# Batch 0's own table of window matmuls, constant products in TensorE's pauses, and the first maxima placed from two queues

## The chip, the cores and the metric

The kernel runs on one core of one Trainium2 chip. The metric is the device time of one execution in microseconds (us), as the median of several runs. In profile rows PE is TensorE's matmul side and PEld its weight loads, DVE is VectorE, ACT is ScalarE, POOL is GpSimd, SP is SyncE; SPq and ACTq are the DMA issues of SP's and ACT's instruction queues.

## The reference, cut to what matters

The whole is one gated cross-attention layer and one mixture-of-experts layer over 16 batches. What the change touches lies in the attention:

```python
# x: (16, 256, 128), ctx: (16, 1601, 128), 16 heads of width 8
qh = einsum('bnd,hde->bhne', layernorm(x), Wq)
kh = einsum('bmd,hde->bhme', ctx, Wk)
vh = einsum('bmd,hde->bhme', ctx, Wv)
att = softmax(einsum('bhne,bhme->bhnm', qh, kh) * 0.125)
out_h = einsum('bhnm,bhme->bhne', att, vh)
...
x = x + tanh(g) * (concat(out_h) @ Wo.T)
x = x + tanh(g2) * moe(layernorm(x))      # top 2 of 8 experts
```

## The kernel before

**Two passes over the scores.** The softmax needs the maximum of each query's row of scores over the 1601 context positions. The kernel computes the scores twice. The first pass makes them with queries on the partitions, in windows of 402 positions: `maximum(G, m)` on TensorE is a pair of `window` matmuls (L770), one for each of two row groups, into one of two PSUM buffers `mxp`, and VectorE reduces the pair with one TENSOR_REDUCE (L1501). A group G is four heads of one batch and has NMX = 16 such pairs; there are 64 groups, four in each batch, and so 1024 pairs. After the 16 pairs of a group VectorE makes the negated maxima `nmx` (L1509), GpSimd splits them into three bfloat16 parts (`split_maxima`, L635 to L641), TensorE turns them (`turn_maxima`, L809), ScalarE copies them to `mxT` (`copy_maxima`, L1122), and two DMAs on SP's queue place them as three more rows of `qpack` (`place_maxima`, L437). The second pass makes the scores with context positions on the partitions (`scores`, L748); those three rows subtract the maximum inside the matmul. ScalarE takes the exponential (L1069), and TensorE multiplies by the values (`weighted`, L796, two units later).

**Units.** The second pass goes in units: 13 tiles of the context for each group, 52 units in a batch, 832 in all. Unit u issues its scores, the windows that a hand-written table `WINDOWS_AT` gives it, and the weighted sums of unit u-2. The table has two rows for each unit: the first pair of row 0 is interleaved with the unit's scores, the pairs of row 1 come after the weighted sums. `issued(u, p)` says how many pairs are out before part p of unit u. In batch 0 some 23 pairs are made ahead of unit 0, and the lead over the table grows from 23 to 30 (`LEAD - max(0, SHORT - u // 3)`); in the other batches it is 30. The same table serves all batches. TensorE's instructions run in program order, and the first unit of each group (units 0, 13, 26, 39 of a batch) waits until the maxima of its group are placed.

**The front.** Ahead of unit 0 TensorE makes keys, queries and the values of batch 0 (`keys` L854, `queries` L838, `values` L868), and then pauses until the keys and queries have been packed by DMA (L383, L389). Between the first 23 pairs it makes the queries and the values of batch 1, whose tiles of 128 positions go four to a PSUM bank (`VCH`).

**SP's queue.** SP issues its DMAs in one written-out order. For the front: packing of batch 0's group 0, context of batch 1, packing of group 1 (12 DMAs), two DMAs of ones (L453), packing of group 2 (12), the maxima of group 0 (2), packing of group 3 (12), packing of batch 1's queries (12, L389), four small loads, two DMAs of ones, the rows of batch 2 (L442). Then comes its loop over the units, in which the maxima of group 1 are placed at unit 9, group 2 at unit 23, group 3 at unit 35, and batch 1's keys are packed at units 14, 23 and 35. At unit 7 ScalarE's `first_keys` of batch 1 waits until all four groups of batch 0 are packed.

Of the kernel before, what the change touches and what calls it, by code (L numbers as in the profile page):

```python
# [16 lines left out]
B, N, D = 16, 256, 128  # L17
# [76 lines left out]
X1_AHEAD, Q1_AHEAD, V1_AHEAD = 1, 2, 8  # L94
# [5 lines left out]
LEAD, SHORT = 30, 7  # L100
WINDOWS_AT = ("1011011110111111111111101001101110011111110111100111",
              "1101111020000000000001101211100011100000011000120000")
PER_BATCH = NG * NMX
ISSUED = [sum(int(WINDOWS_AT[q][r]) for r in range(UNITS) for q in range(2) if 2 * r + q < c)
          for c in range(2 * UNITS)]
# [6 lines left out]
def issued(u, p):  # L112

    b, r = divmod(u, UNITS)
    return LEAD + b * PER_BATCH + ISSUED[2 * r + p] - max(0, SHORT - u // 3)


def windows(u, p):

    to = issued(u, 1) if p == 0 else issued(u + 1, 0)  # L120
    return [divmod(n, NMX) for n in range(issued(u, p), min(to, GROUPS * NMX))]

# [75 lines left out]
def build(nc, x, ctxT, gates, wq, wk, wv, woT, rwT, w1T, w2T, ident, tables, pads, out):  # L198
# [4 lines left out]
    with ctx:  # L203
# [201 lines left out]

        @block.sync
        def _(eng):
# [23 lines left out]
            def place_maxima(G):  # L431
                b, g = divmod(G, NG)
                eng.wait_ge(s_mxT, G + 1)
                rows = KINDS * JJ
                for rg in range(RG):
                    r = rg * RSTEP + MAXROW
                    eng.dma_start(qpack[r:r + KINDS, b % 2, g * JJ:(g + 1) * JJ, :],  # L437
                                  mxT[rg * rows:(rg + 1) * rows, :]).then_inc(s_mxd[G % 2], 16)
# [24 lines left out]
            pack_keys(0, 2)  # L463
            place_maxima(0)
# [266 lines left out]
        def _(eng):  # L731
# [206 lines left out]

            eng.wait_ge(s_wk, 16)
# [7 lines left out]
            for c in range(NV - 1):  # L947
                values(0, c)
            for n in range(issued(0, 0)):
                maximum(*divmod(n, NMX))  # L950
                if n == 0:
                    values(0, NV - 1)
                elif n == X1_AHEAD:
                    turn_rows("X", 1)
                elif n == Q1_AHEAD:
                    queries(1)
                elif V1_AHEAD <= n < V1_AHEAD + VCH[0][1]:
                    values(1, 0, [n - V1_AHEAD])
                elif n == NMX + 1:
                    turn_maxima(0)  # L960
                elif n > NMX + 1 and n - NMX - 1 < NV:
                    values(1, n - NMX - 1)
# [100 lines left out]
        def _(eng):  # L1063
# [93 lines left out]
            copy_maxima(0)  # L1157
            for c in range(1, NV):
# [586 lines left out]
```

## Time and profile before

| | |
|---|---|
| median of 3 runs | 1366.27 us (1364.55 to 1367.53) |
| the profiled execution | 1369.44 us, span 1367.6 us from first to last instruction |
| TensorE busy | 1304.4 us of the span (95%) |
| VectorE busy | 1162.4 us (85%) |
| ScalarE busy | 1097.7 us (80%) |
| mean granted TensorE clock | 0.976 of full |
| first score of unit 0 | 49.07 us into the span |
| first score of batch 1 | 128.8 us |

A profiled execution is one run. The rest of its time over the span (1.8 us) lies before the first and behind the last instruction. The granted clock says at which of its two levels (1.0 is 2.4 GHz, 0.5 is 1.2 GHz) TensorE ran; a stretch with a value between had both.

### The profile page before, as it was taken

Reading aid. Unit: us, or ns where it says so; the run is one execution under the profiler, and the core shown is the slowest. Engines: PE = TensorE matmul, PEld = TensorE weight load, DVE = VectorE, ACT = ScalarE, POOL = GpSimd, SP = SyncE. Lnnn points to the kernel's source line nnn. Section 1 sums busy time; section 2 is a strip of 40 time slices with the busy share of each in tenths; the row PEclk is TensorE's granted clock in tenths of the full one; section 3 lists DMA queues with packets and bytes.
Section 4 is the critical chain, followed back from the end, with each engine's and each line's share of the span. In section 5 each row is a group of like instructions: output and inputs, shape, how many; then the busy total and the mean of one; then the engine's idle time right before and its main releaser. Section 6 shows DMA issues by size and latency. Waiting matters only on the chain.

```text
span 1367.6 us, 37652 instructions
## 1 busy us (share of the span) xinstructions
PE 1304.4 (95%) x13838; PEld 632.2 (46%) x13838; DVE 1162.4 (85%) x2239; ACT 1097.7 (80%) x2170; POOL 550.7 (40%) x1215
## 2 busy tenths in 40 slices
PE   5899999999999999999999999999999999999992
PEld 2334444444444444444444444444444434588881
DVE  7789999999999999999999999999999998354344
ACT  2379898989888898888889898989888889765551
POOL 3033436262626262625253535344444412145442
PEclk7599999999999999999999999999999999999996
DMA  3232121212121212121222122222221210486655
GB/s 113 63 93 79 46 68 50 70 47 71 48 75 47 77 42 82 37 73 46 63 56 63 56 64 61 58 63 59 65 58 36 59 29 2 128 252 201 202 188 202
DMA packets 65762, 109.13 MB, mean 80 GB/s; under 512 B 13660, under 2 KB 36572, under 8 KB 65436
## 3 DMA queue, kind: packets, MB, share of 16 engines
q1 hardware_dynamic: 58804, 94.33, 23.4%
q0 software_dynamic: 4544, 9.45, 2.1%
q10 hardware_dynamic: 2232, 2.96, 0.6%
q8 instruction: 110, 1.80, 0.6%
q14 instruction: 72, 0.59, 0.2%
HBM read 48.81 MB, written 14.64 MB: 46 GB/s over the span
## 4 chain that ended last, share of the span: by engine, by line
PE 78%; DVE 15%; issue 3%; DMA 2%; ACTq 1%; ACT 0%; SPq 0%; POOL 0%; POOLq 0%; DVEq 0%
PE pv L796 28%; PE st L748 14%; PE mxp L770 13%; DVE mx L1501 13%; PE st L1030 5%; PE mxp L1040 5%; PE st L854 4%; PE st L868 3%; PE st L826 1%; PE st L880 1%; DMA arena<-results 1%; PE st L838 1%; PE st L903 1%; PE mxp L1006 1%; PE st L913 1%
## 5 line engine op out<-in xcount | busy, mean ns | idle before, releaser
L1501 DVE TENSOR_REDUCE mx<-mxp 128x2 f32<-128x804 f32 x1024 | 986.1, 988 | 71.3 <-PE mxp L770 59.4
L1069 ACT ACTIVATE arena<-st 128x512 f32<-128x512 f32 (+1 forms) x1664 | 891.9, 595 | 85.1 <-PE st L748 78.8
L796 PE MATMUL pv<-arena 128*32 128x256 f32 x6656 | 533.9, 393 | 0.5 <-ACT pv_sb L1076 0.4
L770 PE MATMUL mxp<-kpack,qpack 48*128 48x402 bf16 x2048 | 464.4, 343 | 24.4 <-DVE mx L1501 15.6
L748 PE MATMUL st<-qpack,kpack 51*128 51x256 bf16 (+1 forms) x3328 | 456.9, 272 | 0.4
L748 PEld LDWEIGHTS st<-qpack,kpack 51*128 51x128 bf16 (+1 forms) x3328 | 200.5, 96 | 208.2 <-ACT arena L1069 113.6
L770 PEld LDWEIGHTS mxp<-kpack,qpack 48*128 48x128 bf16 x2048 | 145.7, 93 | 164.3 <-DVE mx L1501 81.0
L796 PEld LDWEIGHTS pv<-arena 128*32 128x32 f32 x6656 | 131.5, 108 | 176.6 <-ACT arena L1069 90.2
L1205 ACT ACTIVATE arena<-st,bias 128x256 f32<-128x256 f32 x156 | 73.2, 474 | 60.3 <-PE st L1030 39.9
L635 POOL CAST mxs<-nmx 128x8 bf16<-128x8 f32 x64 | 12.2, 191 | 255.2 <-DVE nmx L1509 255.1
L678 POOL DMA_INDIRECT results<-ysb,idx x78 | 74.8, 959 | 90.0 <-PE st L1030 42.2
L668 POOL DMA_INDIRECT rows<-xrow,pos x64 | 66.0, 1031 | 95.3 <-DVE pos L1390 80.0
L1030 PE MATMUL st<-xT,arena 128*128 128x256 f32 x312 | 93.3, 382 | 3.1 <-DMA arena<-in_w1T 1.7
L1040 PE MATMUL mxp<-arena 128*128 128x256 f32 x312 | 92.5, 379 | 0.0
L559 POOL TENSOR_TENSOR tmp<-rstd 128x2 f32<-128x2 f32 x93 | 18.0, 193 | 154.1 <-DVE rstd L1263 149.3
L1111 ACT ACTIVATE arena<-st 128x512 f32<-128x512 f32 x64 | 36.2, 569 | 43.8 <-PE st L868 35.0
L1635 DVE TENSOR_SCALAR ysb<-mxp,xblk,tgate 128x128 f32<-128x128 f32 x78 | 28.4, 406 | 48.4 <-PE mxp L1014 34.7
L854 PE MATMUL st<-arena,wk_sb 128*128 128x400 f32 (+1 forms) x126 | 61.5, 574 | 5.6 <-DMA arena<-in_ctxT 5.6
L868 PE MATMUL st<-wv_sb,arena 128*128 128x128 f32 (+1 forms) x416 | 66.3, 299 | 0.0
L868 PEld LDWEIGHTS st<-wv_sb,arena 128*128 128x128 f32 (+1 forms) x416 | 52.3, 195 | 25.9 <-issue 13.5
L1040 PEld LDWEIGHTS mxp<-arena 128*128 128x128 f32 x312 | 59.0, 189 | 8.2
L610 POOL TENSOR_TENSOR ksp<-kf,ksp 128x400 bf16<-128x400 f32 (+1 forms) x60 | 56.9, 948 | 4.8
(186 smaller groups left out, 942.6 us busy)
## 6 DMA issues: line engine op xcount, KB each, us to landing
kpack<-ksp SPq DMA_DIRECT2D x762, 50.0 KB
arena<-in_ctxT SPq DMA_DIRECT2D x15, 800.5 KB, 4.4
arena<-in_w1T SPq DMA_DIRECT2D x39, 256.0 KB
arena<-in_w2T SPq DMA_DIRECT2D x39, 256.0 KB
qpack<-qsp SPq DMA_DIRECT2D x187, 32.0 KB
xblk<-rows SPq DMA_DIRECT2D x39, 132.0 KB
rows<-in_pads SPq DMA_DIRECT2D x8, 264.0 KB
qpack<-mxT SPq DMA_DIRECT2D x128, 3.0 KB
```

Of the source, the lines that this page charges most:

```text
L668: eng.indirect_dma_start(rows, bass.IndirectOffsetOnAxis(ap=pos[:, k, t:t + 1].bitcast(U32), axis=0), xrow[:, t, k, :], None).then_inc(don ...
L678: eng.indirect_dma_start(results, bass.IndirectOffsetOnAxis(ap=idx[:, i % IDX_BUFS, j:j + 1].bitcast(U32), axis=0), ysb[:, i % YS_BUFS, j, ...
L748: ins = eng.matmul(ring[i][0:n, jj * N:(jj + 1) * N], kpack[rows, b % 2, g * JJ + jj, kt * P:kt * P + n], qpack[rows, b % 2, g * JJ + jj, ...
L770: eng.matmul(mxp[pair % MX_BUFS][:, rg, 0:WIN], qpack[rows, b % 2, g * JJ + jj, t * P:(t + 1) * P], kpack[rows, b % 2, g * JJ + jj, WSTART ...
L796: ins = eng.matmul(pv[32 * j:32 * j + 32, 0:N], vaug[0:n, b % 2, kt, at:at + 32], pt[0:n, (2 * u + rg) % PT_BUFS, jj * N:(jj + 1) * N], st ...
L854: eng.matmul(dst[:, 0:kn], wk_sb[:, :], ctx_sb[:, b % 2, k0:k0 + kn], start=True, stop=True).then_inc(s_kp, 1)
L868: ins = eng.matmul(ring[i][0:n, t * D:(t + 1) * D], ctx_sb[:, b % 2, (t0 + t) * P:(t0 + t) * P + n], wv_sb[:, :], start=True, stop=True)
L1030: eng.matmul(hp[q % HP_BUFS][:, 0:SL], wbuf[:, i % W_BUFS, 0, c * P:(c + 1) * P], xT[:, i % 2, :], start=True, stop=True).then_inc(s_hp, 1)
L1040: eng.matmul(yp[i2 % 2][:, 0:SL], wbuf[:, i2 % W_BUFS, 1, c2 * P:(c2 + 1) * P], hf[:, f % RING, :], start=(c2 == 0), stop=(c2 == HC - 1)). ...
L1069: eng.activation(pt[0:n, c % PT_BUFS, :], ring[bank_of["S", u, p]][0:n, :], ACT.Exp, scale=SCALE).then_inc(s_exp, 1)
L1205: eng.activation(hf[:, q % RING, :], hp[q % HP_BUFS][:, 0:SL], ACT.Gelu_apprx_tanh, bias=bias[:, i % BIAS_BUFS, c:c + 1]).then_inc(s_hg, 1)
L1501: eng.tensor_reduce(mx[:, tj, w, :], mxp[windows_done % MX_BUFS][:, :, 0:WIN], AX.X, ALU.max).then_inc(s_red, 1)
```

## The change

`FIRST_WINDOWS_AT` is a table for batch 0 alone: 22 pairs (`FIRST`) ahead of unit 0, one pair interleaved with unit 0's scores, and all the others (one or two a unit) behind the weighted sums. The other batches keep their table, with a lead of 26 pairs where it was 30. `keep_busy(n)` issues n products of two constant 128 x 128 matrices on TensorE into the bank `pv`, whose content nobody reads: 28 of them after the values of batch 0, and 0 to 2 after each of the first 22 pairs. The values of batch 1 from the second bank on are made two tiles at a time behind pairs 17 to 21, where four followed each other behind one pair. SP places half of group 0's maxima between the fourth and the fifth of the 12 packing DMAs of group 2 (it waits there for `mxT`); ScalarE's queue places the other half right after it has copied them.

```diff
-X1_AHEAD, Q1_AHEAD, V1_AHEAD = 1, 2, 8
+X1_AHEAD, Q1_AHEAD, V1_AHEAD, V1_MORE = 1, 2, 8, NMX + 1
+BUSY_FIRST = 28
-LEAD, SHORT = 30, 7
+FIRST, LEAD = 22, 26
+FIRST_WINDOWS_AT = ("1000000000000000000000000000000000000000000000000000",
+                    "1121121212221112111112112111111111111121122111211112")
 def issued(u, p):
     b, r = divmod(u, UNITS)
-    return LEAD + b * PER_BATCH + ISSUED[2 * r + p] - max(0, SHORT - u // 3)
+    if b == 0:
+        return FIRST + FIRST_ISSUED[2 * r + p]
+    return LEAD + b * PER_BATCH + ISSUED[2 * r + p]
+def beside_first(n):
+    if n == Q1_AHEAD or n > NMX:
+        return 0
+    return 1 if n in (0, X1_AHEAD) or V1_AHEAD <= n < V1_AHEAD + VCH[0][1] else 2
+def first_values(n):
+    if V1_AHEAD <= n < V1_AHEAD + VCH[0][1]:
+        return 0, [n - V1_AHEAD]
+    c, half = divmod(n - V1_MORE, 2)
+    if 0 <= c < NV - 1:
+        first, tiles = 2 * half, VCH[c + 1][1]
+        return c + 1, list(range(first, min(first + 2, tiles)))
+    return None
...
+        def place_half(eng, G, rg):
+            b, g = divmod(G, NG)
+            r, rows = rg * RSTEP + MAXROW, KINDS * JJ
+            eng.dma_start(qpack[r:r + KINDS, b % 2, g * JJ:(g + 1) * JJ, :],
+                          mxT[rg * rows:(rg + 1) * rows, :]).then_inc(s_mxd[G % 2], 16)
...
-            pack_keys(0, 2)
-            place_maxima(0)
+            pack_keys(0, 2, range(2))
+            eng.wait_ge(s_mxT, 1)
+            place_half(eng, 0, 0)
+            pack_keys(0, 2, range(2, PARTS))
             pack_keys(0, 3)
             pack_queries(1)
...
+            def keep_busy(times):
+                for _ in range(times):
+                    eng.matmul(pv[:, 0:D], wk_sb[:, :], wq_sb[:, :], start=True, stop=True)
...
+            keep_busy(BUSY_FIRST)
             for n in range(issued(0, 0)):
                 maximum(*divmod(n, NMX))
+                keep_busy(beside_first(n))
...
-                elif V1_AHEAD <= n < V1_AHEAD + VCH[0][1]:
-                    values(1, 0, [n - V1_AHEAD])
...
-                elif n > NMX + 1 and n - NMX - 1 < NV:
-                    values(1, n - NMX - 1)
+                if first_values(n):
+                    values(1, *first_values(n))
...
             copy_maxima(0)
+            eng.wait_ge(s_mxT, 1)
+            place_half(eng, 0, 1)
```

## Rows read from the trace of the kernel before

**Rows 1.** The page: TensorE's total, and its granted clock in 40 equal slices.

```profile
PE 1304.4 (95%) x13838; PEld 632.2 (46%) x13838; DVE 1162.4 (85%) x2239; ACT 1097.7 (80%) x2170; POOL 550.7 (40%) x1215
...
PEclk7599999999999999999999999999999999999996
```

**Rows 2.** Busy time in stretches: from:to, length, busy us (instructions), clock, DMA share, GB/s.

```profile
18.60:23.20 4.60, 0.00 (x0) 0.00 (x0) 3.54 (x2) 1.53 (x3) 2.35 (x6) 0.50 0.45 100
23.20:49.30 26.10, 21.30 (x81) 9.63 (x81) 20.69 (x24) 4.08 (x10) 2.92 (x8) 0.51 0.31 93
...
52.70:59.50 6.80, 6.80 (x51) 2.12 (x51) 4.87 (x6) 3.29 (x7) 0.00 (x0) 0.53 0.22 56
...
63.00:69.80 6.80, 6.80 (x46) 2.28 (x43) 3.74 (x5) 3.51 (x7) 0.72 (x2) 0.53 0.35 76
...
78.43:128.80 50.37, 48.11 (x582) 18.84 (x578) 48.37 (x66) 43.38 (x86) 12.87 (x37) 1.00 0.29 89
128.80:199.47 70.67, 70.27 (x820) 30.82 (x817) 66.32 (x120) 63.01 (x124) 27.14 (x71) 1.00 0.19 56
```

**Rows 3.** Timeline, all engines: start, us, engine, line, operation, count, idle before and releaser.

```profile
12.74 2.84 PE L868 MATMUL st<-wv_sb,arena 128*128 128x128 f32 x24
...
17.91 3.72 ACTq L389 DMA_DIRECT2D qpack<-qsp  x5
...
23.25 0.59 PE L770 MATMUL mxp<-kpack,qpack 48*128 48x402 bf16 x2 [7.66 <-DMA qpack<-qsp]
...
82.61 11.08 DVE L1501 TENSOR_REDUCE mx<-mxp 128x2 f32<-128x804 f32 x12
```

**Rows 4.** Timeline: the maxima of group 0 on VectorE and on ScalarE.

```profile
40.57 0.24 DVE L1509 TENSOR_REDUCE nmx<-mx 128x4 f32<-128x16 f32 x2
...
42.45 0.37 ACT L1122 ACTIVATE mxT<-st 12x256 bf16<-12x256 f32 x1 [5.43 <-PE st L809]
```

**Rows 5.** Timeline of SP's queue: start, us in which SP issues, count.

```profile
31.43 11.89 SPq L383 DMA_DIRECT2D kpack<-ksp  x12
43.37 1.53 SPq L437 DMA_DIRECT2D qpack<-mxT  x2
44.94 7.85 SPq L383 DMA_DIRECT2D kpack<-ksp  x12
...
64.56 3.23 SPq L442 DMA_DIRECT2D x_sb<-in_x  x1
70.43 1.48 SPq L437 DMA_DIRECT2D qpack<-mxT  x2
...
92.81 1.56 SPq L437 DMA_DIRECT2D qpack<-mxT  x2
94.42 15.68 SPq L383 DMA_DIRECT2D kpack<-ksp  x24
110.14 1.51 SPq L437 DMA_DIRECT2D qpack<-mxT  x2
```

**Rows 6.** Timeline of TensorE: unit 0, units at half clock, units and keys at full clock.

```profile
49.07 0.27 PE L748 MATMUL st<-qpack,kpack 51*128 51x256 bf16 x1
...
55.76 1.08 PE L796 MATMUL pv<-arena 128*32 128x256 f32 x8
...
57.64 1.09 PE L796 MATMUL pv<-arena 128*32 128x256 f32 x8
...
72.45 0.94 PE L854 MATMUL st<-arena,wk_sb 128*128 128x400 f32 x2
...
84.73 0.34 PE L770 MATMUL mxp<-kpack,qpack 48*128 48x402 bf16 x2
...
86.53 0.28 PE L748 MATMUL st<-qpack,kpack 51*128 51x256 bf16 x1
...
87.59 0.28 PE L748 MATMUL st<-qpack,kpack 51*128 51x256 bf16 x1
...
96.42 0.20 PEld L748 LDWEIGHTS st<-qpack,kpack 51*128 51x128 bf16 x4 [0.28 <-DMA qpack<-mxT]
```

More of the change, by code:

```diff
@@ L99 @@
 ROWS_AT, LAST_ROWS_AT = {1: 40, 2: 42, 3: 44}, {9: 0, 12: 1, 15: 2, 18: 3}
-LEAD, SHORT = 30, 7
+FIRST, LEAD = 22, 26
 WINDOWS_AT = ("1011011110111111111111101001101110011111110111100111",
               "1101111020000000000001101211100011100000011000120000")
+FIRST_WINDOWS_AT = ("1000000000000000000000000000000000000000000000000000",
+                    "1121121212221112111112112111111111121122111211112112")
 PER_BATCH = NG * NMX
-ISSUED = [sum(int(WINDOWS_AT[q][r]) for r in range(UNITS) for q in range(2) if 2 * r + q < c)
-          for c in range(2 * UNITS)]
+ISSUED, FIRST_ISSUED = [[sum(int(at[q][r]) for r in range(UNITS) for q in range(2) if 2 * r + q < c)
+                         for c in range(2 * UNITS)] for at in (WINDOWS_AT, FIRST_WINDOWS_AT)]
 def key_rows(kt):
@@ L431, in place_maxima @@
             def place_maxima(G):
-                b, g = divmod(G, NG)
                 eng.wait_ge(s_mxT, G + 1)
-                rows = KINDS * JJ
                 for rg in range(RG):
-                    r = rg * RSTEP + MAXROW
-                    eng.dma_start(qpack[r:r + KINDS, b % 2, g * JJ:(g + 1) * JJ, :],
-                                  mxT[rg * rows:(rg + 1) * rows, :]).then_inc(s_mxd[G % 2], 16)
+                    place_half(eng, G, rg)
             def load_rows(b):
```

## Prediction

> **What bounds the kernel now.** I read the page first. TensorE is busy 95% of the span and its granted clock is 9 or more tenths in all slices but the first two and the last [rows 1]. Then the table of stretches. From 128.80 to 199.47 us, which is batch 1, TensorE is busy 70.27 of 70.67 us at full clock, VectorE 66.32 [rows 2]: in the 15 later batches TensorE's work sets the time, and the change leaves that work as it is. So the result hangs on one question: how much earlier does batch 1 begin than at 128.80, and what is paid back at the end.
>
> Before that point there are three stages. From 18.6 to 23.2 TensorE has nothing, since the queries are still being placed, and its clock falls to 0.50. From 23.2 to 49.3 it stays at 1.2 GHz. From 49.3 to 69.8 it changes between the levels (0.53 in two stretches of 6.8 us in which TensorE is busy without a break), and only from 69.8 on does it stay at 2.4 GHz [rows 2]. Unit 0 begins at 49.07 [rows 6]. From unit 13 (78.43) to batch 1 (128.80) VectorE is busy 48.37 of 50.37 us: there VectorE's maxima set the pace, not TensorE. Last I read SP's queue, since each group of 13 units waits for its maxima from there: it issues almost without a pause from 31.43 to 67.79 [rows 5].
>
> **The 28 products and the ones between pairs.** A value matmul has the shape of a `keep_busy` product. Twelve took 2.84 us at full clock, 0.24 each [rows 3]. 28 take 6.6 us, from 15.6 to 22.2. The first pair starts at 23.25, released by the last query DMA (issued until 21.63, landed 1.6 later) [rows 3], so the products cost nothing; at half clock they would take 13.3 and cost 5.7, but the clock was at full when the values ended. After a pair one or two products follow: 0.34 for the pair [rows 6] and 0.48 make 0.82, under the 0.92 to 0.93 that VectorE needs for one maximum (11.08 for 12) [rows 3]. Hidden, again only at full clock.
>
> The Trainium skill (TensorE: Matmul & The Clock Gate, "HAM oscillation — how this bites in real kernels") says that a wait for a DMA between bursts of matmuls puts the clock back to its lower level and that the burst behind it runs cold. The fall in the empty stretch from 18.6 agrees [rows 2]. By that rule the 28 products do what is wanted, and any new DMA wait further on undoes it.
>
> **The front at full clock.** First maximum on VectorE at 23.6, 16 of them at 0.93 end at 38.5, `nmx` at 38.8 (it was 40.81). From there to the end of the copy to `mxT` took 2.0 (42.82) [rows 4], so `mxT` is there at 40.8. SP has by then issued the four first DMAs of group 2 (12 took 11.89, 12 others 7.85 [rows 5], so about 4 us of stall behind the ones and 0.65 each: until 38.1) and waits. The two halves go out at once on two queues and land about 3.0 after the start: bounds are 3.6 (92.81 to 96.42, where unit 26 waited 0.28) and 2.8 (110.14 to 112.9, where unit 39 didn't wait) [rows 5, 6]. That is 43.9. TensorE's own path through pairs 17 to 21 with two value tiles each ends there too: VectorE's maximum 18 starts near 41.3, since the turn and the values stand before its pair, and three more at 0.93 and the last pair give 43.8. **Unit 0 at 44, 5 us earlier.** The second queue saves one issue, 0.77 (half of 1.53) [rows 5]. The Trainium skill (DMA: Bandwidth & Descriptors, "Issuing engines are not separate DMA queues") says that a second issuing engine saves only the issuing time; by it the sum is the same.
>
> **Units 0 to 12.** The table gives 10 pairs to units 0 to 6; VectorE sets 0.93 each, so unit 7 is at 53. Units 7 to 12: six units at 1.06 (86.53 to 87.59), ten pairs at 0.2 to 0.34, four chunks of keys at 0.94, one turn: 12.5 [rows 6]. At unit 7 ScalarE's copy of the first key chunk waits for the last packing of group 3. That ends 8 x 0.65 + 7.85 after SP's half (41.7), at 54.8, and lands 1.6 later: 1.4 us of wait. TensorE would be ready for unit 13 at 67.
>
> **What is late next: SP's queue.** Unit 13 needs the maxima of group 1. They are issued at unit 9 of SP's loop, behind everything of the front. Before, SP began with group 3 at 44.94 and ended the load of batch 2's rows at 67.79 (64.56 + 3.23): 22.85. It then waited until 70.43 for `mxT` [rows 5]. After the change SP sits idle from 38.1 to 40.9 and has eight packing DMAs left over: 40.9 + 0.77 + 5.2 + 22.85 = **69.8**, two us later than before, though TensorE asks ten us earlier. With 3.0 to land: 72.8. A second issue stall behind the two DMAs of ones (the 4 us above against 2.8 in the 3.23) may be left over: 0 to 1.3, I take 0.7. **Unit 13 at 73.5**, bounds 72.4 and 75; before 78.43. Gain here 4.9. TensorE idles for some 6.5 us in front of it, more than the 4.6 of rows 2's first stretch, and the clock should fall.
>
> **The cold stretch.** Twice before, the clock was back after 6.8 us of unbroken work [rows 2]. A unit with one pair takes 1.88 at half clock (55.76 to 57.64) [rows 6], one with two more, some 1.95 in the mean; at full clock the units of batch 0 take 1.29 in the mean (50.37 over 39). 6.8 x (1 - 1.29 / 1.95) = 2.3 us lost; bounds 0 (the clock holds) and 6 (two such stretches and part of a third).
>
> **Units 13 to 51.** Before: 50.37 for 49 pairs. Now 48 pairs. To unit 22: 11 pairs where there were 13, at most 1.9 less; TensorE is then nearly the bound, I take 0.8 less. Units 22 to 39: 19 pairs where there were 21, but SP needs 17.33 from the placing of group 2 to that of group 3 (92.81 to 110.14, 24 packing DMAs in between, no pause) and unit 39 started 2.8 after it: the same 22.4 as before, nothing gained. Units 39 to 51: 18 pairs where there were 15; VectorE needs 18 x 0.93 and 0.24: 17.0 against 15.9, 1.1 more. Together 50.7, bounds 49.5 and 52. **Batch 1 at 73.5 + 2.3 + 50.7 = 126.5, 2.3 us earlier.**
>
> **The later batches and the end.** Four pairs fewer are ahead. The nearest place is the turn of group 3's maxima at unit 34, for which 70 pairs of the batch's count are out where 64 are needed, so the lead of 26 costs nothing there; bound 0.3 a batch. The four pairs come in the last batch instead, into units that had no maxima: 0 to 0.34 each, I take 0.5 in all. Net **1.8 us** earlier. The profiled execution took 1369.44 (span 1367.6 and 1.8 around it), 3.2 over the median; the difference carries over: 1369.44 - 1.8 = 1367.6 for it, 1366.27 - 1.8 = **1364.5** for the median.
>
> **Rivals.**
> A, the forecast: SP's queue holds unit 13 and the clock falls once. 1362.8 to 1366.5. Chance 0.47.
> B, SP holds unit 13, but the clock is kept or comes back at once, because TensorE arrives late (keys, the wait at unit 7). Without the 2.3: 1362.2, with the low bounds of landing and units 1360. For it: between 49.3 and 69.8 the clock rose three times; against: the wait is longer than the one at 18.6. Chance 0.2.
> C, SP's queue isn't what holds unit 13: unit 13 at 67, no cold stretch, 11.4 earlier instead of 4.9 and 2.3 more: 1366.3 - 11.4 + 0.3 + 0.5 = 1356. It needs SP's issues to shrink, against 0.65 in every packing DMA. Chance 0.07.
> D, slower: after the idle wait at unit 13 the clock stays at half for long, as it did from 23.2 to 49.3 with TensorE 82% busy [rows 2]; the new table spreads its pairs thinly. Each us at half clock costs 0.34. Without any the gain is 4.1; from 12 us on it is gone, at 20 it is 0.2% slower, at 26 us 4.7 more: 1371. Chance 0.14.
> E, the change doesn't do what it says: the clock falls between 15 and 44 in spite of the products. At half clock a pair and two products take 0.52 + 0.96 against 0.93 of VectorE: 0.55 for each of some eight pairs, 4.4 us, on SP's chain one to one: about 1366 to 1369. For it: pairs with one value each from 31 to 36 did not raise it, in the second stretch of that table [rows 2]. Chance 0.12.
>
> **Range and chances.** 1360 to 1368.5 holds A, B, most of E and the near end of D. The forecast's own range is 1362.8 to 1366.5. A measurement of this kernel can tell about 0.2% (2.7 us) from no change. Faster by more: B nearly whole, C and a fifth of A, plus little: 0.37. Slower by more: most of D, a little of E: 0.13. Within: 0.50.
>
> **What would show it.** Clock 1.00 from 15.6 to 44; pairs 0.93 apart; the first score of unit 0 near 44; SP's placing of group 1 at 69.8 with no idle time ahead of it; TensorE idle before unit 13 with the DMA of `mxT` as releaser, for about 6 us; clock 0.5 behind it; batch 1 at 126.5 and batches of 70.6 after. The forecast is wrong if SP's placing comes well ahead of 69, if the clock holds at unit 13, or if batches 1 to 14 are no longer 70.6 long.

## The result and the profile after

The change made the kernel slower: 1390.37 us median (1388.56 to 1393.08, four runs) beside 1366.24 (1364.55 to 1367.53) for the kernel before on the same chip, ratio 1.0179 [1.0159, 1.0199], 24.1 us. The forecast was 1364.5, with 1360 to 1368.5 as its range. A ratio here and below is worked out from the runs and not from the two medians; a run more than 1.5% above the fastest of its kernel is left out of it, which is one run in all, 1383.59 of `ones_earlier`. In the diff ahead of the prediction the second string of `FIRST_WINDOWS_AT` is wrong from unit 35 on and has 66 pairs, where the kernel that ran has 67:

```python
FIRST_WINDOWS_AT = ("1000000000000000000000000000000000000000000000000000",
                    "1121121212221112111112112111111111121122111211112112")
```

The profiled execution took 1393.08 us, span 1391.2, against 1369.44 and 1367.6. First the page, which answers to [rows 1].

```profile
PE 1334.8 (96%) x13946; PEld 647.8 (47%) x13946; DVE 1167.0 (84%) x2239; ACT 1097.7 (79%) x2170; POOL 549.6 (40%) x1215
...
PEclk8589999999999999999999999999999999999996
```

TensorE has 108 matmul instructions more (54 products in two parts each) and 30.4 us more of busy time. Of these, 23.7 lie ahead of batch 1 and 6.1 in batches 1 to 14. Products at full clock would account for 54 x 0.23 = 12.4 us; the rest of the 23.7 is work that ran at the lower clock, which now fills most of the second slice (34.8 to 69.6). Next the table of stretches of the kernel after; its columns are those of [rows 2].

```profile
18.60:23.20 4.60, 2.89 (x25) 2.52 (x24) 3.27 (x2) 1.72 (x3) 1.96 (x4) 1.00 0.42 91
24.40:57.10 32.70, 32.58 (x124) 20.12 (x125) 20.56 (x23) 3.16 (x7) 2.92 (x8) 0.50 0.18 52
57.10:65.30 8.20, 8.07 (x59) 2.64 (x60) 6.15 (x7) 5.72 (x11) 0.00 (x0) 0.50 0.28 81
83.90:142.40 58.50, 55.78 (x577) 19.16 (x577) 46.03 (x62) 43.44 (x85) 8.30 (x30) 0.84 0.29 90
142.40:214.60 72.20, 70.89 (x818) 30.76 (x815) 67.52 (x121) 62.32 (x123) 27.10 (x72) 1.00 0.19 55
214.60:286.20 71.60, 70.76 (x822) 30.78 (x819) 66.71 (x120) 62.84 (x124) 31.01 (x74) 1.00 0.21 59
```

Two things stand out. The products did keep the clock at 1.00 over the stretch where it had fallen before (18.6 to 23.2), but 1.2 us later it fell all the same and stayed at 0.50 until 65.3, through unit 0 and beyond. And a batch at full clock now lasts 71.6 us where it lasted 70.7 [rows 2].

The ledger from the first scores of the units (read from both traces, us into the span):

| | before | after | adds |
|---|---|---|---|
| unit 0 | 49.1 | 57.1 | |
| unit 13 | 78.4 | 83.9 | |
| batch 1 | 128.8 | 142.4 | 13.6 |
| batch 15 (14 batches later) | 1116.7 | 1143.4 | 13.1 |
| last unit | 1179.3 | 1206.2 | 0.2 |
| end of the span | 1367.6 | 1391.2 | -3.3 |

So there are two losses of nearly the same size, one in the front and one spread over batches 1 to 14. The last line is work of the mixture of experts that the change doesn't touch; in the traces of the experiments it takes 186 to 190 us without any order, so I take it for the spread between executions. The front differs between executions too. `before` and two kernels of the experiments (`lead26_before`, `lead26_pool_order`) have the same instructions on TensorE up to unit 10, and their traces have unit 0 at 49.1, 48.4 and 51.5. So up to 3 us between single traces of a front can't be read as an effect.

**The front.** Timeline of the kernel after, all engines, in the columns of [rows 3].

```profile
14.73 6.42 PE L971 MATMUL pv<-wq_sb,wk_sb 128*128 128x128 f32 x56
...
22.86 0.43 PE L798 MATMUL mxp<-kpack,qpack 48*128 48x402 bf16 x2 [1.71 <-DMA qpack<-qsp]
...
28.47 0.52 PE L798 MATMUL mxp<-kpack,qpack 48*128 48x402 bf16 x2
28.92 1.22 PE L971 MATMUL pv<-wq_sb,wk_sb 128*128 128x128 f32 x4
29.05 0.99 DVE L1537 TENSOR_REDUCE mx<-mxp 128x2 f32<-128x804 f32 x1 [0.60 <-PE mxp L798]
...
30.07 0.52 PE L798 MATMUL mxp<-kpack,qpack 48*128 48x402 bf16 x2
...
47.68 0.24 DVE L1545 TENSOR_REDUCE nmx<-mx 128x4 f32<-128x16 f32 x2
```

The 28 products end at 21.15 and the first pair starts at 22.86: TensorE still has 1.71 us with nothing to do. Once the clock is down, a pair and its two products take 1.60 us (28.47 to 30.07), and VectorE, which used to set the pace at 0.93, waits 0.6 for each pair. The `nmx` that was foretold for 38.8 comes at 47.68. Before the change the same pairs, without products, gave it at 40.57 though the clock was at half there too [rows 4]: at half clock the products are not filler, they are the bound. Unit 0 then doesn't wait for its maxima (placed from 50.53 on): TensorE comes to it at 57.05 straight out of pairs 17 to 21 and their value tiles, which also run 1.60 us apart.

**SP's queue**, in the columns of [rows 5], and unit 13 on TensorE:

```profile
50.53 0.76 SPq L433 DMA_DIRECT2D qpack<-mxT  x1
51.33 13.02 SPq L406 DMA_DIRECT2D kpack<-ksp  x20
64.39 7.86 SPq L412 DMA_DIRECT2D qpack<-qsp  x12
...
76.55 3.09 SPq L468 DMA_DIRECT2D x_sb<-in_x  x1
79.69 2.98 SPq L433 DMA_DIRECT2D qpack<-mxT  x2
...
83.88 0.69 PE L776 MATMUL st<-qpack,kpack 51*128 51x256 bf16 x4 [4.44 <-DMA qpack<-mxT]
```

The queue waits for `mxT` (copied at 50.50, not 40.8) and then issues almost without a pause; it gets to group 1's maxima 29.2 us later, where 28.8 were foretold (40.9 to 69.8). This part of the reading was right, it only began ten us late.

### The profile page after: what moved, and what is told of

It reads as the page before. It is cut to its first block, busy times and chain, and to the rows that moved or that the text cites. A ratio compares the mean times of both kernels' runs of the same rounds, so it can differ in the third digit from the quotient of the medians.

```text
span 1391.2 us, 37868 instructions
## 1 busy us (share of the span) xinstructions
PE 1334.8 (96%) x13946; PEld 647.8 (47%) x13946; DVE 1167.0 (84%) x2239; ACT 1097.7 (79%) x2170; POOL 549.6 (40%) x1215
## 4 chain that ended last, share of the span: by engine, by line
PE 69%; DVE 20%; SPq 4%; issue 4%; DMA 2%; ACT 1%; ACTq 1%; POOL 0%; POOLq 0%; DVEq 0%
PE pv L824 24%; DVE mx L1537 17%; PE st L776 12%; PE mxp L798 12%; PE st L1064 5%; PE mxp L1074 4%; PE st L882 4%; PE st L896 2%; SPq L406 2%; PE pv L971 1%; PE st L854 1%; PE st L908 1%; PE st L931 1%; PE st L941 1%; PE mxp L1040 1%
## 5 line engine op out<-in xcount | busy, mean ns | idle before, releaser
L798 PE MATMUL mxp<-kpack,qpack 48*128 48x402 bf16 x2048 | 457.8, 344 | 17.1 <-DVE mx L1537 13.6
L798 PEld LDWEIGHTS mxp<-kpack,qpack 48*128 48x128 bf16 x2048 | 142.4, 93 | 170.8 <-DVE mx L1537 85.3
L663 POOL CAST mxs<-nmx 128x8 bf16<-128x8 f32 x64 | 12.2, 191 | 435.8 <-DVE nmx L1545 435.7
L1241 ACT ACTIVATE arena<-st,bias 128x256 f32<-128x256 f32 x156 | 73.7, 475 | 56.1 <-PE st L1064 53.7
L706 POOL DMA_INDIRECT results<-ysb,idx x78 | 74.8, 959 | 87.8 <-PE st L1064 46.7
L896 PEld LDWEIGHTS st<-wv_sb,arena 128*128 128x128 f32 (+1 forms) x416 | 52.6, 195 | 24.7 <-issue 13.1
L633 POOL TENSOR_TENSOR kf<-kf,ksp 128x400 f32<-128x400 f32 (+1 forms) x60 | 56.6, 944 | 5.0
```

The costliest lines, as they stand in the source:

```text
L706: eng.indirect_dma_start(results, bass.IndirectOffsetOnAxis(ap=idx[:, i % IDX_BUFS, j:j + 1].bitcast(U32), axis=0), ysb[:, i % YS_BUFS, j, ...
L798: eng.matmul(mxp[pair % MX_BUFS][:, rg, 0:WIN], qpack[rows, b % 2, g * JJ + jj, t * P:(t + 1) * P], kpack[rows, b % 2, g * JJ + jj, WSTART ...
L896: ins = eng.matmul(ring[i][0:n, t * D:(t + 1) * D], ctx_sb[:, b % 2, (t0 + t) * P:(t0 + t) * P + n], wv_sb[:, :], start=True, stop=True)
L1241: eng.activation(hf[:, q % RING, :], hp[q % HP_BUFS][:, 0:SL], ACT.Gelu_apprx_tanh, bias=bias[:, i % BIAS_BUFS, c:c + 1]).then_inc(s_hg, 1)
```

## Experiments

Medians stand beside that of the kernel before on the same chip. Experiments on different chips are compared by their differences to it: 24.1 us for the changed kernel. In the edits `+` and `-` are against the kernel named, and `...` marks what is left out. A start of a unit and a stretch of the clock are from one profiled execution each.

### The two losses apart

**1. `lead26_before`: the kernel before with the lead of 26 alone.**

```diff
-LEAD, SHORT = 30, 7
+LEAD, SHORT = 26, 3
```

> The kernel before with a lead of 26 pairs instead of 30 in all batches (the front keeps its 23 pairs); nothing else is changed. Theory L (the shorter lead delays the maxima of each group, and behind them in GpSimd's queue the counts that TensorE waits for near unit 46): batches 1 to 14 become 71.55 us long instead of 70.63, the time 1366.2 + 13 = about 1378 us. Rival R (the lead is harmless, and the later batches were longer for another reason, such as the state in which batch 0 hands over): batches stay at 70.6, 1364 to 1367 us.

Measured: 1381.52 (1380.60 to 1382.38) beside 1368.03, ratio 1.0106 [1.0089, 1.0123]. Batch 1 begins at 127.5, and each batch from 1 to 13 lasts 71.53 to 71.56 us where it lasted 70.62 to 70.67:

```profile
127.50:199.00 71.50, 70.65 (x820) 30.73 (x816) 66.61 (x120) 62.77 (x124) 27.11 (x72) 1.00 0.19 55
```

The lead costs 0.92 us a batch by itself, 12.2 us from batch 1 to batch 15 in this trace.

**2. `lead30_after`: the changed kernel with a lead of 30**, the four extra pairs at units 26, 29, 31 and 33 of batch 0.

```diff
-FIRST, LEAD = 22, 26
+FIRST, LEAD = 22, 30
...
```

> The changed kernel with a lead of 30 in batches 1 to 15; the four more pairs are made in batch 0 behind units 26, 29, 31 and 33. Theory L: batches 1 to 14 are 70.6 again, batch 0 is up to 3.7 us longer: 1390.4 - 13 + 1 to 4 = 1378 to 1381 us. Rival R: batches 1 to 14 stay near 71.5, 1390 us or more.

Measured: 1380.00 (1378.97 to 1381.04) beside 1368.03, ratio 1.0094 [1.0077, 1.0111]. Batch 1 begins at 140.2, unit 0 at 57.9; a batch lasts what it did before:

```profile
210.80:281.40 70.60, 70.26 (x821) 30.95 (x816) 66.38 (x120) 62.85 (x124) 31.05 (x73) 1.00 0.21 60
```

Both directions agree: 12.2 us of the 24.1 go with the lead (24.1 - 12.0; 13.5 in `lead26_before`), and most of what remains sits ahead of batch 1.

**3. `no_products`: the changed kernel without `keep_busy`.**

```diff
-            keep_busy(BUSY_FIRST)
...
-                keep_busy(beside_first(n))
```

> The changed kernel without any of the constant products; table, lead, values two tiles at a time and the two queues stay. Theory P (in the changed kernel the clock fell at 24.7 us, and from there each pair with its products took 1.60 us at half clock where VectorE needs 0.99): the maxima of group 0 are copied near 42 us instead of 50, SP places group 1 near 71, batch 1 begins near 130 instead of 142.4, and 1378 to 1380 us. Rival (the front was late because of the table or of SP's wait): batch 1 still begins after 138, 1386 us or more.

Measured: 1384.24 (1383.10 to 1386.11) beside 1368.03, ratio 1.0126 [1.0109, 1.0143]. Unit 0 begins at 49.0, unit 13 at 75.5, batch 1 at 129.7. The clock is at half from 17.3 to 54.8, and yet the front is 8 us shorter at unit 0 than with the products (57.1). So the products cost 8 us there rather than saving 5, and 7.9 us of the median (24.1 less 16.2 over the kernel before). Batch 1 begins near 130, as the expectation had it; the time is 4 us above it. The lead and the products together make some 20 of the 24.1 us; the other 4 no run takes apart.

**4. `long_first`: 36 products where there were 28**, so that they reach up to the first pair.

```diff
-BUSY_FIRST = 28
+BUSY_FIRST = 36
```

> The changed kernel with 36 products ahead of the first pair instead of 28, so that TensorE has no pause before 22.9 us. Theory P (the clock fell because of the 1.7 us pause and the thin first pairs): the clock stays at full through the front, pairs come 0.93 apart, group 0 is copied at 41, SP places group 1 at 69.8, TensorE then idles before unit 13 and the clock falls there, batch 1 begins near 126.5, later batches are 71.55: 1376 to 1378 us. Rival P2 (between the first three pairs there is too little for TensorE in any case): the clock falls near 24 to 28, 1386 to 1391 us.

Measured: 1387.95, 1380.48, 1394.91 and 1383.45, median 1385.70 beside 1368.03, ratio 1.0139 [1.0087, 1.0190]; the expectation was 1376 to 1378. In the profiled execution (1387.95) there is no pause ahead of the first pair, and the clock stays at 1.00 from 8.8 to 66.8. TensorE and SP in that trace:

```profile
14.59 8.20 PE L971 MATMUL pv<-wq_sb,wk_sb 128*128 128x128 f32 x72
22.72 0.42 PE L798 MATMUL mxp<-kpack,qpack 48*128 48x402 bf16 x2
...
73.71 0.68 PE L776 MATMUL st<-qpack,kpack 51*128 51x256 bf16 x4 [8.39 <-DMA qpack<-mxT]
74.32 1.08 PE L824 MATMUL pv<-arena 128*32 128x256 f32 x8
```

```profile
40.51 0.76 SPq L433 DMA_DIRECT2D qpack<-mxT  x1
...
69.51 2.98 SPq L433 DMA_DIRECT2D qpack<-mxT  x2
```

This is the front that was foretold, to a few tenths: `mxT` at 40.5 (40.8), unit 0 at 44.0 (44), SP at group 1's maxima at 69.5 (69.8), unit 13 at 73.7 (73.5), TensorE idle in front of it for 8.4 us. What was not foretold stands in its table of stretches:

```profile
67.20:84.30 17.10, 10.59 (x84) 2.93 (x84) 5.39 (x6) 5.71 (x12) 1.88 (x3) 0.51 0.50 156
84.30:110.60 26.30, 24.41 (x302) 8.96 (x294) 25.02 (x37) 22.84 (x45) 5.48 (x22) 1.00 0.17 48
110.60:125.20 14.60, 14.56 (x102) 4.48 (x106) 7.94 (x13) 7.29 (x14) 0.12 (x1) 0.53 0.35 108
```

The clock comes back not 6.8 us after unit 13's start but 10.2 us (83.9), and it falls a second time at unit 39, which waited 1.06 us for its maxima, for another 13.6 us. Batch 1 begins at 133.8. That is later than the 129.7 of `no_products`, which has unit 0 and unit 13 later (49.0 and 75.5) but only the first of the two falls: the clock that was held up to unit 13 is all given back behind it, and the median is no better either (1385.70 and 1384.24).

### What holds units 13 and 26

**5. `busy_at_waits`: `long_first`, and products put in front of the waits of units 13 (28) and 39 (12)**, into the bank that the scores overwrite.

```diff
+BUSY_AT = {13: 28, 39: 12}
...
+                eng.wait_ge(*freed[i])
+                for _ in range(BUSY_AT.get(u, 0) if rg == 0 else 0):
+                    eng.matmul(ring[i][:, 0:D], wk_sb[:, :], wq_sb[:, :], start=True, stop=True)
...
-                eng.wait_ge(*freed[i])
```

> As long_first, with 28 products in front of the wait of unit 13 and 12 in front of that of unit 39, into the bank that the unit's scores then overwrite. SP's order stays. Theory C (the fall of the clock in those waits, not the waits themselves, is what made batch 1 begin at 133.8 instead of 126.5): unit 13 still starts at 73.7, the clock stays at full from 9 us on, batch 1 begins near 124 to 126, 1376 to 1378 us. Rival (the waits themselves cost it): batch 1 still after 131, 1383 us or more.

Measured: 1379.41, 1377.86, 1379.12 and 1392.56, median 1379.27 beside 1367.47, ratio 1.0123 [1.0078, 1.0169]. The profiled execution has the clock at 1.00 from 9.5 us to the experts' part. Unit 13 begins at 74.7 and batch 1 at 127.2, a little later than the 124 to 126 expected. By these two traces the falls in `long_first` cost 133.8 - 127.2 = 6.6 us; the medians are 5.9 us apart when each is taken over its kernel before.

The products do not reach the end of either wait here. Ahead of the first pair TensorE has nothing to do for 0.40 us, and ahead of unit 13 for 2.06:

```profile
66.13 6.52 PE L775 MATMUL st<-wq_sb,wk_sb 128*128 128x128 f32 x56
74.71 0.48 PE L779 MATMUL st<-qpack,kpack 51*128 51x256 bf16 x4 [2.06 <-DMA qpack<-mxT]
```

The clock held through both, while 1.06 us ahead of unit 39 in `long_first` and 1.71 us ahead of the first pair in the changed kernel were followed by a fall. So the length of a rest alone does not decide.

**6. `place1_early`: `long_first`, with group 1's maxima placed ahead of the packing of batch 1's queries.**

```diff
-            pack_queries(1)
...
+            place_maxima(1)
+            pack_queries(1)
...
-                if r in PLACE_AT and b * NG + PLACE_AT[r] < GROUPS:
+                if r in PLACE_AT and 1 < b * NG + PLACE_AT[r] < GROUPS:
```

> As long_first (36 products, no pause ahead of the first pair), and SP places the maxima of group 1 before it packs batch 1's queries and before its second two DMAs of ones and the load of batch 2's rows. Theory Q (SP's order holds unit 13 at 73.7 us, and the idle wait there drops the clock for 17 us): group 1 is placed near 57.5 to 59, unit 13 starts at 65 to 67 with the clock still full, batch 1 begins 8 to 16 us earlier than the 133.8 of long_first, 1371 to 1377 us. Rival (unit 13 isn't held by SP alone, or the clock falls anyway and the time is given back): unit 13 before 68, but batch 1 after 129, 1382 us or more.

Measured: 1378.46 (1377.73 to 1379.70) beside 1367.47, ratio 1.0092 [1.0076, 1.0108]. Unit 13 begins at 65.2, without a wait; batch 1 at 125.2. SP's queue was what held unit 13: in `long_first` these maxima were copied at 57.6 and placed from 69.51 on. But the wait is only passed on. SP now comes to group 2's maxima at 83.11, copied at 77.6, and TensorE stands in front of unit 26:

```profile
80.24 0.64 PE L825 MATMUL pv<-arena 128*32 128x256 f32 x8
80.81 0.34 PE L799 MATMUL mxp<-kpack,qpack 48*128 48x402 bf16 x2
87.56 0.68 PE L777 MATMUL st<-qpack,kpack 51*128 51x256 bf16 x4 [6.40 <-DMA qpack<-mxT]
88.17 1.08 PE L825 MATMUL pv<-arena 128*32 128x256 f32 x8
```

The weighted sums behind it take 1.08 us for eight where they took 0.64 ahead of it: the clock fell in the wait, as at unit 13 before.

**7. `two_queues_only`: the kernel before with group 0's maxima placed from two queues**, nothing else of the change.

```diff
-            pack_keys(0, 2)
-            place_maxima(0)
+            pack_keys(0, 2, range(2))
+            eng.wait_ge(s_mxT, 1)
+            place_half(eng, 0, 0)
+            pack_keys(0, 2, range(2, PARTS))
...
+            eng.wait_ge(s_mxT, 1)
+            place_half(eng, 0, 1)
```

> The kernel before, with only the placing of group 0's maxima changed: half from ScalarE's queue, half from SP's after four of the 12 packing DMAs of group 2. By the sum in the prediction SP reaches the maxima of group 1 two us later (69.8 instead of 67.8), where they are not copied before 70.4: no change, 1366 to 1368 us. Rival (SP's later DMAs matter, or the half queue saves something at unit 0): unit 0 or unit 13 moves by over 1 us.

Measured: 1367.70 (ten runs, 1364.84 to 1371.04) beside 1367.47, ratio 1.0007 [0.9992, 1.0022]. No difference. SP comes to group 1's maxima at 70.21. In its trace unit 13 does begin 3.5 us earlier than in the kernel before (74.9), which is the sign of the rival; but so it does in `lead26_before` (74.6), which has no such placing, and from the first pair to unit 0 it takes 25.8 us in both kernels (22.26 to 48.09 and 23.25 to 49.07). So it is the spread between executions.

**8. `queue_lead30`: `place1_early` with the lead of 30, and batch 1's third key packing moved behind the placing of group 3.**

```diff
-FIRST, LEAD = 22, 26
+FIRST, LEAD = 22, 30
...
-                        pack_keys(1, 2)
...
+                        pack_keys(1, 2)
```

> As place1_early, and the lead is 30 again (four more pairs in batch 0, behind units 26, 29, 31, 33), and SP packs group 2 of batch 1's keys behind the maxima of group 3 instead of ahead of them. Theory (three causes: clock in the front, SP's order, lead): batches 1 to 14 are 70.6, no wait at units 13 and 39, batch 1 begins near 118 to 121 against 128.8 in the kernel before, 1356 to 1360 us. Rival (VectorE's pace in batch 0 or a further clock fall takes it back): batch 1 at 127 or later, 1364 us or more.

Measured: 1368.91 (eleven runs, 1366.65 to 1373.75) beside 1367.47, ratio 1.0011 [0.9998, 1.0024]. The kernel is back at the time of before, with a front in which unit 0 begins at 44.3, unit 26 at 87.8 (it waited 5.06 us for its maxima) and batch 1 at 128.4, after a wait of 1.40 us for its own first maxima. Batch 1 lasts 73.74 where it lasted 70.67. The 1356 to 1360 that were hoped for are missed.

### Where the front can still go

**9. `queue_spread`: the packing of batch 1 cut up and the ones moved**, so that no placing stands behind a whole round of packing.

```diff
-            ones_rows(1)
...
-                        pack_keys(1, 0)
+                        pack_keys(1, 0, range(PARTS // 2))
...
+                        pack_keys(1, 0, range(PARTS // 2, PARTS))
...
+                        ones_rows(1)
```

> As queue_lead30 (36 products, lead 30, group 1 placed early), with SP's DMAs of batch 0 in another order: the maxima of group 2 are placed after half of the packing of batch 1's group 0 instead of all of it, the two DMAs of ones for batch 1 go behind the maxima of group 3, the load of batch 2's rows directly behind the packing of the queries. Theory Q (in batch 0 SP's issue time of 0.65 us a DMA, in the order in which it was written, is what each group's first unit waits for, first at unit 13, then at unit 26): unit 26 starts at 81 to 83 instead of 87.8, the clock doesn't fall in the waits, batch 1 begins near 116 to 119, 1356 to 1360 us. Rival (the wait moves on to unit 39 or 52, as it moved from 13 to 26): batch 1 after 124, 1364 us or more.

Measured: 1368.13 beside 1365.57, ratio 1.0057 [1.0025, 1.0089]; again the rival and not the theory. The twelve runs fall into two groups: seven from 1363.7 to 1368.2 and five from 1379.3 to 1383.3. In the profiled one (1366.00) units 13, 26 and 39 no longer wait; unit 52, the first of batch 1, waits 5.4 us and begins at 124.7. Its maxima were copied at 114.1 and placed from 120.74 on, so SP's queue is late once more.

**10. `spread_no_products`: the same without products.**

> As queue_spread without any constant products. It tells what the products are worth once SP's order no longer takes it back. Theory: the front runs at half clock, group 0 is copied at 42 instead of 40 and unit 0 starts at 49 instead of 44; batch 1 begins 3 to 6 us after that of queue_spread, 1360 to 1365 us. Rival (VectorE or SP sets batch 0 in any case): within 1 us of queue_spread.

Measured: 1370.98 (ten runs, 1368.25 to 1375.41) beside 1365.57, ratio 1.0041 [1.0028, 1.0054], above the 1360 to 1365 expected. In the profiled execution the first pair came late, at 25.69, and unit 0 begins at 51.8. The runs no longer fall into two groups; they lie between those of `queue_spread`. Against the medians of the two groups (1367.35 and 1380.79) the products gain 3.6 us in one course and cost 9.8 in the other.

**11. `ones_earlier`: `queue_spread` with the ones sent at round 23, and 2, 2 and 1 products beside the first three pairs where there were 1, 1 and 0.** (The expectation calls this thinned; it is three products more.)

```diff
-    if n == Q1_AHEAD or n > NMX:
+    if n > NMX:
         return 0
-    return 1 if n in (0, X1_AHEAD) or V1_AHEAD <= n < V1_AHEAD + VCH[0][1] else 2
+    return 1 if n == Q1_AHEAD or V1_AHEAD <= n < V1_AHEAD + VCH[0][1] else 2
...
+                        ones_rows(1)
...
-                        ones_rows(1)
```

> The changed kernel with LEAD 30, long products in front, and SP's queue spread as in queue_spread; beyond it the ones rows of batch 1's last group are sent at round 23, so that they no longer stand between two packings of maxima at round 35, and the products beside the front's pairs are thinned to 2, 2 and 1. If SP's queue is what still holds unit 52 (it placed batch 1's group 0 at 120.7 us in queue_spread, and the unit began at 124.7), the placing comes 3 to 4 us earlier, unit 52 starts at 118 to 121, batch 1 lasts 71 to 72 us instead of 74.7, and the median is 1357 to 1362. If the wait only moves on to another packing (unit 39, or batch 1's group 3), or the clock falls elsewhere in the front, the median stays at 1364 or above, as in queue_spread.

Measured: 1365.36 (twelve runs, 1361.07 to 1383.59) beside 1367.70, ratio 0.9984 [0.9964, 1.0004]. The first theory's 1357 to 1362 is missed in the median; only three of twelve runs are under 1362.1. The profiled execution is the slowest of the twelve, and for that reason the most telling one. The same 36 products stand ahead of the first pair in `queue_spread`; here are the two beside each other, `queue_spread` first:

```profile
14.87 8.20 PE L973 MATMUL pv<-wq_sb,wk_sb 128*128 128x128 f32 x72
23.01 0.43 PE L800 MATMUL mxp<-kpack,qpack 48*128 48x402 bf16 x2
...
24.00 0.34 PE L800 MATMUL mxp<-kpack,qpack 48*128 48x402 bf16 x2
```

```profile
14.93 8.20 PE L973 MATMUL pv<-wq_sb,wk_sb 128*128 128x128 f32 x72
25.87 0.59 PE L800 MATMUL mxp<-kpack,qpack 48*128 48x402 bf16 x2 [2.74 <-DMA qpack<-qsp]
...
27.97 0.52 PE L800 MATMUL mxp<-kpack,qpack 48*128 48x402 bf16 x2
```

In this execution the packed queries landed at least 2.9 us later, TensorE stood for 2.74 us, the pairs are 2.1 us apart instead of 1.0 (the one product more beside the first has a part in that), and from 26.0 to 70.4 the clock is at half. It fell 0.13 us into the first pair, ahead of the products in which the two kernels differ:

```profile
40.00:50.00 10.00, 10.00 (x39) 6.29 (x38) 5.98 (x7) 0.66 (x1) 0.00 (x0) 0.50 0.00 0
50.00:62.20 12.20, 12.20 (x48) 7.62 (x46) 7.70 (x10) 1.70 (x3) 0.80 (x4) 0.50 0.11 31
```

Unit 0 begins at 62.2 instead of 44.3, and 13.5 us of that are left at batch 1 (138.2 and 124.7). The late landing is not the products' doing: two kernels without any, `spread_no_products` and `lead26_pool_order`, have it in their traces (first pair at 25.69 and 26.24) and unit 0 at 51.8 and 51.5, some 3 us later than in the others without products (48.1 to 49.1). With the products the same delay costs 18. The mean granted clock goes the same way in all runs of the two kernels: 0.985 to 0.991 in those under 1370, 0.971 to 0.977 in those above 1376. None of the 68 runs of the kernel before beside these experiments is above 1372.1, so the second course belongs to the kernels with products. The 1394.91 of `long_first` (clock 0.973) and the 1392.56 of `busy_at_waits` (0.978) look like it; they were not traced. In the better half of its executions (1361.07 to 1363.98) this is the fastest kernel of the study; in the median it can't be told from the kernel before. Products that reach on behind the latest landing were not tried.

### The lead, once more

**12. `lead26_pool_order`: `lead26_before`, with GpSimd splitting the queries of two batches on before it waits for the next batch's first maxima.**

```diff
-                if b + 1 < B:
-                    split_maxima(b * NG + 4)
...
+                if b + 1 < B:
+                    split_maxima(b * NG + 4)
```

> As lead26_before, and GpSimd splits the maxima of the next batch's group 0 behind the split of the queries instead of ahead of it. Theory G (with the lead of 26 GpSimd waits four pairs longer for those maxima, so its split of the queries moves under VectorE's L1361, which takes 0.608 us instead of 0.356 there, and the ranks that TensorE's turn waits for come later: 0.5 of the 0.92 us a batch): batches 1 to 14 become 71.0 us, the time 1381.5 - 7 = about 1374 us. Rival (the later end of the maxima themselves is what TensorE waits for near unit 47): batches stay 71.5 or get longer, 1380 us or more.

Measured: 1376.97 (1374.65 to 1381.56) beside 1365.57, ratio 1.0082 [1.0057, 1.0108]; a batch lasts 71.13 where `lead26_before` has 71.55 and the kernel before 70.63. So the order on GpSimd is 0.42 of the 0.92. (By the medians over the kernel before, 13.5 and 11.4 us, only 2.1 us come back where 13 batches make 5.5; the intervals reach 2.3 and 3.5 us to either side.) Timeline of GpSimd and VectorE around it, first in the kernel before, then in `lead26_before`:

```profile
679.56 0.19 POOL L635 CAST mxs<-nmx 128x8 bf16<-128x8 f32 x1 [5.11 <-DVE nmx L1509]
...
685.04 0.40 POOL L617 CAST qsp<-qf 128x256 bf16<-128x256 f32 x1 [2.97 <-ACT qf L1088]
```

```profile
690.04 0.19 POOL L635 CAST mxs<-nmx 128x8 bf16<-128x8 f32 x1 [10.12 <-DVE nmx L1509]
...
691.16 0.39 POOL L617 CAST qsp<-qf 128x256 bf16<-128x256 f32 x1
```

With four pairs fewer ahead, `nmx` of the next batch's first group comes later in the batch. GpSimd runs in program order and stands in front of it for 10.1 us instead of 5.1, so the split of the queries behind it, ready by then, starts 1.1 us later in the batch (691.16 - 628.3 = 62.9 against 685.04 - 623.2 = 61.8). It then overlaps VectorE's small steps of the routing. One of them, of two elements on each partition, is in the rows of one source line (min, median, max in ns), before and in `lead26_before`:

```profile
L1361 DVE TENSOR_TENSOR xrow<-top x3: 349/354/359, 616.4 to 757.7; 128x2 f32<-128x2 f32 x3
```

```profile
L1361 DVE TENSOR_TENSOR xrow<-top x2: 606/609/612, 621.4 to 692.9; 128x2 f32<-128x2 f32 x2
```

With the order turned it takes 0.15:

```profile
694.67 0.67 POOL L623 TENSOR_TENSOR qsp<-qf,qsp 128x256 bf16<-128x256 f32 x1
695.28 0.15 DVE L1361 TENSOR_TENSOR xrow<-top 128x2 f32<-128x2 f32 x1
```

The first scores of batch 8's units tell where the time goes. With the shorter lead, in the changed kernel as in `lead26_before`, unit 32 takes 0.32 us longer, unit 35 0.11 and unit 47, where TensorE takes up the routing, 0.54. With the order turned, 0.47 of those 0.54 are gone, while the 0.3 and 0.11 at units 32 and 35 stay. So GpSimd's order is what costs at unit 47. The other 0.5 us a batch isn't settled: at units 32 and 35 the later `nmx` falls among other small operations of VectorE, which is argued from the order of the trace; no run took it apart.

## Why the prediction was wrong

**"28 take 6.6 us, from 15.6 to 22.2 ... so the products cost nothing."** The size was right (6.42); they ended 1 us early (21.15). What was missing is the pause that stays behind them. 1.0 us was foretold (22.2 to 23.25) and passed over; it was 1.71. At this place the clock held in the five traces with a pause of 0 or 0.40 us, and fell and stayed down in the three with 1.61 (`lead30_after`), 1.71 and 2.74. `queue_spread` and `ones_earlier` have the same 36 products and differ in this by when a DMA landed, which speaks for the pause and not the number of products; it rests on one trace of each. The length of the pause is not the whole of it, as `busy_at_waits` shows (2.06 us ahead of unit 13, no fall). The Trainium skill (TensorE: Matmul & The Clock Gate, "HAM oscillation — how this bites in real kernels") says that a wait for a DMA puts the clock back; the prediction drew the rule in for new waits further on, and not for the rest of the old one. The section tells of waits longer than that rest. The runs agree with it at units 13 and 26 (8.39 us in `long_first`, 6.40 in `place1_early`); that a rest of 1.71 us can be followed by a fall is shown by the runs here alone.

**"The front at full clock", unit 0 at 44.** This is the step that failed: 57.1. It was rival E that came, with a chance of 0.12 and at the wrong price. E priced 0.55 us for each of some eight pairs, 4.4 in all. In fact every pair from the fourth on took 1.60 where 0.93 were expected (`nmx` 8.9 us late), the turn and pairs 17 to 21 with their values made it 13 at unit 0, and the clock stayed down for 41 us. E's reason, that pairs with small work between them do not raise the clock, was in [rows 2] already: 26 us at half clock with TensorE 82% busy. The prediction used that row for D and trusted full clock in its sum. By single traces the front's 13.6 us come apart as 8.6 for the clock up to unit 13 and what follows (142.4 against 133.8 in `long_first`), 6.6 for the falls at units 13 and 39 (133.8 against 127.2 in `busy_at_waits`), less 1.6 (127.2 against 128.8), which is within the spread of such traces, so that a gain of the new order is not shown. Taken the other way, leaving the products out gives 12.7 of it back (129.7). The forecast's own gain, a front at full clock up to unit 13 and one fall behind it, came in `long_first` and was worth nothing: batch 1 at 133.8 where 126.5 was foretold.

**SP's queue.** Right, in its place and in its size: 69.8 foretold, 69.5 in `long_first`, once `mxT` came on time; `place1_early` takes it away and unit 13 begins at 65.2 (rival C had 67 for that). So was the second queue's small part in the sum (0.77 us): it measured no difference by itself.

**"6.8 x (1 - 1.29 / 1.95) = 2.3 us lost."** Right mechanism, wrong size. The stretch at half clock was 17 us in `long_first`, of which TensorE stood for 6.5, and there was a second one of 13.6 at unit 39, where the wait was only 1.06 us. Together 6.6 us. Two stretches of 6.8 us in which the clock was between its levels did not show how long it stays down when it has fallen for good; this is rival D in two pieces. D's 0.34 for each us of work at half clock would make 8 of the 24 us of work in them.

**"Units 13 to 51 ... together 50.7, bounds 49.5 and 52."** Too low. In `busy_at_waits`, at full clock throughout and with the same table, they took 52.5 (74.7 to 127.2). The prediction took VectorE's maxima as what sets the pace before; but TensorE is busy 48.11 of the 50.37 us there and VectorE 48.37 [rows 2], so neither is clearly the bound, and in the 52.46 us of `busy_at_waits` TensorE is busy 50.61 (2.94 of them the products ahead of unit 39) and VectorE 45.34.

**"So the lead of 26 costs nothing there; bound 0.3 a batch."** The second step that failed: 0.92 a batch, 12 to 13 us in all, and `lead26_before` shows it alone. The count of pairs against the turn of group 3 was right, and is not where it costs. The prediction looked only at TensorE's needs. A smaller lead moves `nmx` on VectorE and with it everything that stands in line behind it on GpSimd, which is shown for 0.42 of the 0.92; the rest is open. The row for that was there to be asked for: GpSimd in front of `nmx`, 5.1 us idle with the split of the queries in line behind it.

**The last batch and the sum.** 0.5 foretold, 0.2 measured, which tells little: the last batch takes 62.8 to 64.6 us in the traces with the lead of 26. The sum of what failed: 126.5 against 142.4 at batch 1, and 13.1 where nothing was put.

## What to carry to other kernels

A filler that is to hold the clock is best made to reach the instruction that ends the wait, in the slowest execution and not in the mean one: rests of 1.61 to 2.74 us behind it were followed by a fall at the first pair here, though one of 2.06 was not at unit 13. Price it at the lower clock too, since if the clock falls anyway the filler becomes the bound. And see what the clock it holds is worth at the next deadline before paying for it: unit 0 came 5 us earlier in `long_first` than in `no_products`, and batch 1 no earlier at all. When a table moves work in time, follow for each engine that runs in program order what stands behind the moved result, also on engines that are half idle. When a wait is taken from a queue that issues without a pause, the next wait on that queue takes its place: count the issues up to each of the following deadlines before the first is moved.

## What the runs showed of the hardware

- TensorE at half clock did not come back although it had no gap: 32.58 of 32.70 us busy from 24.4 to 57.1 in the kernel after, 22.2 of 22.2 from 40.0 to 62.2 in `ones_earlier`. In the kernels before and after, `no_products` and `ones_earlier` alike it rose only at unit 0 or some 6 to 8 us behind its start.
- Rests of TensorE of 1.06, 1.61, 1.71 and 2.74 us were followed by a fall of the clock (unit 39 in `long_first`; the first pair in `lead30_after`, the changed kernel and `ones_earlier`), rests of 0.40 and 2.06 us in `busy_at_waits` were not.
- One and the same program had two courses: twelve executions of `queue_spread` lie in two groups 13 us apart. `ones_earlier`, which is the same up to the first pair, showed the slower course in a trace: a DMA that landed at least 2.9 us later moved unit 0 by 18. Without products such a landing moved it by some 3.
- A VectorE operation on two elements a partition took 0.15, 0.35 or 0.61 us, by how it lay beside GpSimd's operations.
- SP's issues behind the two DMAs of ones were slow: 3.09 us for the load of a batch's rows that took 0.44 elsewhere, then 2.98 for two placings that took 1.5 elsewhere (kernel after; alike in `no_products` and `long_first`). The prediction put 0.7 for this leftover; it was 1.5.
